# Ternary weights of a four-layer kernel prepared beside the first attention instead of ahead of it

## The reference

```python
x = norm(x + attention(x, wq, wk, wv, wo))          # causal, 32 query heads, 8 key heads, 16 wide, rotary
x = norm(x + ternary_ffn(x, w_fc, w_proj))          # 512 -> 2048 -> 512
x = norm(x + linear_attention(x, ...))
x = norm(x + experts(x, ...))                       # 16 experts, 2 per row, and a shared one

def ternarize_weights(w):                           # once for w_fc (2048x512), once for w_proj (512x2048)
    gamma = mean(abs(w))
    return sign(round(w / (gamma + 1e-6))) * gamma
```

## Time and profile before

| | us |
|---|---|
| median of 3 runs | 1881.5 (1878.66 to 1881.55) |
| the profiled execution | 1877.94 |
| its span in the profile | 1876.0 |
| mean granted TensorE clock | 0.952 |
| TensorE, VectorE, ScalarE, POOL busy | 86%, 64%, 50%, 22% |

### The profile page before, as it was taken

One profiled execution on the slowest core, in us unless ns is written; L12 is line 12 of the kernel. 1 busy time (PEld: TensorE's weight loads), 2 busy tenths in 40 slices (PEclk: granted clock), 3 DMA queues, 4 the chain that ended last, 5 costly groups with the idle time before them and its releaser, 6 DMA issues. The chain is left out here.

```text
span 1876.0 us, 33875 instructions
## 1 busy us (share of the span) xinstructions
PE 1616.8 (86%) x12714; PEld 817.7 (44%) x12714; DVE 1199.5 (64%) x2028; ACT 936.7 (50%) x1624; POOL 419.6 (22%) x503
## 2 busy tenths in 40 slices
PE   0488999978799998599996999777896999999997
PEld 0363333326333333244442454444553555666564
DVE  2556898844589885699975787699451243333277
ACT  4344677734467774577763666355221333333332
POOL 0070000116100002122222222255153111111154
PEclk9798999989899999899998999899897999999999
DMA  9000000000000000356454999543062564646344
GB/s 333 1 2 1 2 2 2 2 1 1 1 2 2 2 2 1 85 112 125 98 99 155 349 358 346 190 148 117 18 112 50 207 238 137 193 153 201 107 128 135
DMA packets 153970, 197.80 MB, mean 105 GB/s; under 512 B 94042, under 2 KB 97336, under 8 KB 151120
## 3 DMA queue, kind: packets, MB, share of 16 engines
q1 hardware_dynamic: 142288, 168.08, 29.1%
q0 software_dynamic: 7344, 20.73, 4.1%
q10 hardware_dynamic: 4176, 6.82, 1.0%
HBM read 184.94 MB, written 56.40 MB: 129 GB/s over the span
## 5 line engine op out<-in xcount | busy, mean ns | idle before, releaser
L713 ACT ACTIVATE attn_prob<-attn_ps_t 128x512 f32<-128x512 f32 x576 | 312.6, 595 | 151.2 <-PE attn_ps_t L667 149.7
L737 DVE TENSOR_REDUCE attn_mx<-attn_ps_s 128x2 f32<-128x1024 f32 (+3 forms) x304 | 342.7, 1163 | 42.9 <-PE attn_ps_s L648 39.4
L1985 PE MATMUL sparse_ps_g<-wgate,sparse_xT 128*128 128x352 f16 x1128 | 186.3, 316 | 3.6 <-DVE sparse_xT L2063 3.6
L680 PE MATMUL attn_ps_o<-attn_prob,V 128*32 128x256 f32 x2304 | 175.1, 389 | 0.8 <-ACT attn_oT L721 0.8
L1985 PEld LDWEIGHTS sparse_ps_g<-wgate,sparse_xT 128*128 128x128 f16 x1128 | 105.6, 99 | 75.2 <-DVE sparse_xT L2063 24.8
L1134 PE MATMUL lin_ps_z<-arena,lin_xT 128*128 128x512 f16 x576 | 134.0, 383 | 0.9 <-DVE lin_relu L1278 0.9
L900 PE MATMUL ffn_ps_fc<-wfcT,ffn_xT 128*128 128x512 f16 x512 | 115.8, 386 | 16.6 <-DMA ffn_xT<-ffn_x 16.6
L667 PE MATMUL attn_ps_t<-arena,KT 64*128 64x256 f16 x1152 | 112.5, 274 | 12.3 <-DMA arena<-attn_mT 6.5
L910 PE MATMUL ffn_ps_y<-wprojT,ffn_hT 128*128 128x512 f16 x512 | 115.1, 384 | 8.0 <-DMA ffn_hT<-ffn_h 8.0
L648 PE MATMUL attn_ps_s<-KT,arena 64*128 64x512 f16 (+3 forms) x768 | 115.8, 337 | 2.1 <-DVE attn_mx L737 2.1
L789 POOL TENSOR_TENSOR attn_o<-O,attn_o 128x512 f16<-128x512 f32 x16 | 18.5, 1158 | 442.3 <-ACT attn_o L726 442.3
(11 more groups left out here) (301 smaller groups left out, 3044.3 us busy)
## 6 DMA issues: line engine op xcount, KB each, us to landing
wgate<-gate_d SPq DMA_DIRECT2D x47, 1408.0 KB
wdown<-down_d SPq DMA_DIRECT2D x47, 768.0 KB
lin_sp_raw<-in_L_ffn_w_gate_up_dram SPq DMA_DIRECT2D x56, 352.0 KB, 5.3
gate_d<-lin_sp_parts SPq DMA_DIRECT2D x56, 352.0 KB, 4.9
y_d<-y SPq DMA_DIRECT2D x47, 256.0 KB
down_d<-lin_sp_parts SPq DMA_DIRECT2D x42, 256.0 KB, 5.1
lin_sp_raw<-in_L_ffn_w_down_dram SPq DMA_DIRECT2D x28, 256.0 KB, 5.2
prep_w_fc<-in_L_ffn_w_fc_dram SPq DMA_DIRECT2D x4, 1024.0 KB, 14.9
```

What stands on the lines that cost most here:

```text
L680: last = pe.matmul(ps_o[32 * jj:32 * jj + 32, 256 * half:256 * half + 256], V[:, kt, 4 * jg + jj, :], prob[(2 * q + jj // 2) % 4][:, half, ...
L713: act.activation(prob[g % 4][:, par, :, :], ps_t[:, (2 * g + par) % 3, :, :], ACT.Exp, scale=HD ** -0.5).then_inc(exp_done, 1)
L737: dve.tensor_reduce(mx[x % 2][:, c, :, at:at + per], ps_s[:, 2 * (r % 2):2 * (r % 2) + 2, 0:per * n].rearrange("p e (h k) -> p e h k", k=n ...
L1985: last = pe.matmul(ps_g[u][n][rows, :], xT[u][:, a, k, rows], w, start=(k == 0 and i == 0), stop=(k == KC - 1 and i == 2), skip_group_chec ...
```

## The change

The preparation block keeps only the tables, x and attention's weights. x is loaded by SP in four-tile pieces; the block waits for the first batch's half of it, the second half has a semaphore that the second projection waits for. ScalarE's wait for the weights is split: wq, wk, wv first, wo by itself.

In the first projection SP loads both ternary matrices in 16 chunks of 128x1024 (512 KB), with four buffers that lie in the place of `m.wfcT`; ScalarE sums the absolute values of two chunks per tile, as the last part of its list with a lag of 1; at the end TensorE adds the 16 sums and VectorE works out gamma and the thresholds.

In the first attention the chunks are loaded a second time, one per unit, by SP, after the unit's four small transfers. POOL compares each in three instructions (is less, is greater, difference), all sixteen chunks ahead of the rest of its stream. SP waits for each result, one unit later, and transposes it by DMA (two transfers for a chunk of w_fc, one for one of w_proj). The transposes and copies by TensorE and ScalarE are gone. The second batch's blocks are unchanged but for the wait for x.

```diff
@@ load_and_prepare
-                for c in range(4):
-                    sp.dma_start(w_fc[:, c * C4:(c + 1) * C4, :], fc_rows[:, c * C4:(c + 1) * C4, :]).then_inc(fc_in[c], 16)
-                for c in range(4):
-                    sp.dma_start(w_proj[:, c, :], proj_rows[:, c, :]).then_inc(proj_in[c], 16)
+                for t in range(0, TB, 4):
+                    sp.dma_start(m.X[:, t:t + 4, :], rows[:, t:t + 4, :]).then_inc(first_in, 16)
+                sp.dma_start(m.X[:, TB:NT, :], rows[:, TB:NT, :]).then_inc(m.later_in, 16)
+                sp.wait_ge(first_in, 32)
...
-                act.dma_start(w_o[:, :, :], d["L0_attn_wo"].rearrange("(k p) n -> p k n", p=P)).then_inc(wa_in, 16)
-                act.dma_start(m.X[:, :, :], d["L0_attn_x"].rearrange("b (t p) n -> p (b t) n", p=P)).then_inc(x_in, 16)
+                act.dma_start(w_o[:, :, :], d["L0_attn_wo"].rearrange("(k p) n -> p k n", p=P)).then_inc(wo_in, 16)
...
-                act.wait_ge(wa_in, 64)
+                act.wait_ge(wa_in, 48)
                 act.activation(m.wqkv_h[:, :, :], w_qkv[:, :, :], ACT.Copy, scale=WS).then_inc(hi_done, 1)
+                act.wait_ge(wo_in, 16)
                 act.activation(m.wo_h[:, :, :], w_o[:, :, :], ACT.Copy, scale=WS).then_inc(hi_done, 1)
...
+CHUNK = 2 * D
+CHUNKS = 2 * D * FF // (P * CHUNK)
@@ project_qkv
+                if b == 0:
+                    for c in range(CHUNKS):
+                        after(sp, abs_done, c - 3)
+                        rows = ternary_rows(d, c)
+                        sp.dma_start(raw[:, c % 4, :].rearrange("p (n k) -> p n k", n=rows.shape[1]), rows).then_inc(raw_in[c % 4], 16)
+                else:
+                    sp.wait_ge(m.later_in, 16)
...
+                def sums(t, u):
+                    if b == 0 and t == TB - 1:
+                        pe.wait_ge(abs_done, CHUNKS)
+                        pe.wait_ge(v_done, TB)
+                        pe.matmul(ps_v[:, 0:CHUNKS], m.ones[:, :], part[:, :], start=True, stop=True).then_inc(sum_done, 1)
...
-                run_tiles(act, TB, [(0, xhi), (2, vals), (2, qhi), (3, evac)])
+                def size(t, u):
+                    if b == 0:
+                        for c in range(t * CHUNKS // TB, (t + 1) * CHUNKS // TB):
+                            act.wait_ge(raw_in[c % 4], 16 * (c // 4 + 1))
+                            act.activation(raw[:, c % 4, :], raw[:, c % 4, :], ACT.Abs,
+                                           accum_out=part[:, c:c + 1]).then_inc(abs_done, 1)
+
+                unrolled(TB, [(0, of(xhi)), (2, of(vals)), (2, of(qhi)), (3, of(evac)), (1, of(size))])
@@ attend
             @block.gpsimd
             def _(pool):
+                def chunk(c):
+                    u, w = c % 2, c // (CHUNKS // 2)
+                    pool.wait_ge(raw_in[u], 16 * (c // 2 + 1))
+                    after(pool, turned[u], 16 * turns[c])
+                    pool.tensor_scalar(tern[u][:, :], raw[u][:, :], m.thr[:, 1, w:w + 1], None, ALU.is_lt).then_inc(neg_done, 1)
+                    pool.tensor_scalar(raw[u][:, :], raw[u][:, :], m.thr[:, 0, w:w + 1], None, ALU.is_gt).then_inc(neg_done, 1)
+                    pool.wait_ge(neg_done, 2 * c + 2)
+                    pool.tensor_tensor(tern[u][:, :], raw[u][:, :], tern[u][:, :], ALU.subtract).then_inc(tern_done, 1)
+
+                if ternary:
+                    for c in range(CHUNKS):
+                        chunk(c)
                 for kind, *a in ORDER:
...
+                def turn(sp, c):
+                    sp.wait_ge(tern_done, c + 1)
+                    columns = ternary_columns(m, c)
+                    for n, out in enumerate(columns):
+                        size = CHUNK // len(columns)
+                        sp.dma_start_transpose(out=out, in_=tern[c % 2][:, n * size:(n + 1) * size]).then_inc(turned[c % 2], 16)
+
                 for x, (qt, jg) in enumerate(UNITS):
                     sp.wait_ge(mt_done, x + 1)
                     for i in range(4):
                         at = qt * P + 32 * i
                         sp.dma_start(QT[3 * HD:P:64, 8 * jg:8 * jg + 8, at:at + 32],
                                      mT[x % 2][32 * i:32 * i + 16, :]).then_inc(mt_in[x % 2], 16)
+                    if ternary and x < CHUNKS:
+                        after(sp, tern_done, x - 1)
+                        rows = ternary_rows(d, x)
+                        sp.dma_start(raw[x % 2][:, :].rearrange("p (n k) -> p n k", n=rows.shape[1]), rows).then_inc(raw_in[x % 2], 16)
+                        if x:
+                            turn(sp, x - 1)
+                if ternary:
+                    turn(sp, CHUNKS - 1)
+                    for u in range(2):
+                        sp.wait_ge(turned[u], 16 * sum(len(ternary_columns(m, c)) for c in range(u, CHUNKS, 2)))
```

127 lines of the change are left out of this document (48 added, 79 removed).

## The result

The changed kernel took 1861.65 us in the median of four runs (1859.3 to 1864.9), the kernel before 1880.08 in the four beside them (1878.5 to 1881.6): a ratio of 0.9909 (95% interval 0.9889 to 0.9929), 18.4 us less. That is faster, by 0.9%, and 4.7 us above the 1857 of the forecast. A second measurement of the same kernel, the last of the experiments, gave 0.9942 (0.992 to 0.9965), which is 10.9 us. The forecast had 24, a ratio of 0.987.

A forecast was written before the change was run, and what follows sets the result against it. Barrier-ended stages bound the kernel: preparation is a gapless chain, attention a TensorE stage with POOL idle. -54.3 + 9.0 + 3.6 + 13.6 + 2 + 2 = -24.1 us, so 1857 us; range 1840 to 1878.

The forecast's parts named there:

- T: POOL's time per chunk in the first attention: two comparisons of 1.95 us and a subtraction of 2.3, 6.2 us (4.2 to 12.9).
- Preparation: Block before the first projection: it ends with wo's low part at 25.0 us, projection starts at 27.2 instead of 81.5, -54.3 us.
- Measuring in the ring: First projection: ScalarE's measuring lengthens each tile's chain of evacuation, x cast, POOL's rows and q cast; +9.0 us (0 to 13).
- Rival C: First projection: longer tiles drop TensorE to 1.2 GHz, costing 24 us in six tiles; 1881 us, no change; chance 0.06.
- rival B: First attention: POOL becomes the bound if T reaches about 12.7 us; slower than before, 1900 us at T = 15; chance 0.11.
- The comparison: POOL in the first attention: comparing 1024 columns with a scalar per partition takes 1.95 us, close under the cast's rate.
- rival A: POOL in the first attention: a comparison at nearly one column per cycle, 0.95 us, T 4.2; 1852 us; chance 0.17.
- SyncE's queue: First attention: unit 2's rows, and TensorE with them, wait behind chunk 0's compare and transpose; +3.6 us (1.6 to 22).
- one term for the clock: First attention: after the hole TensorE starts at the lower level, four us at half rate; +2 us (0 to 4).
- The end: End of the first attention: the last chunk's comparing delays POOL's low parts and TensorE's transpose; +13.6 us (11.6 to 20).
- The port: First attention: VectorE's small rows wait for POOL instructions at the shared port; +2 us (0 to 6); big reductions spared.

The follow-up runs named there:

- one_comparison: The changed kernel with the second comparison of each chunk left out (weights come out wrong); ratio 0.9891 to the kernel before, attention 288.9 us.
- ring_order: The changed kernel with ScalarE's two absolute sums per tile moved ahead of its cast of the queries; ratio 0.9874 to the kernel before, first projection 68.6 us.
- quarter_pieces: ring_and_table with each of POOL's three operations of a chunk cut into four of 256 columns; ratio 0.9736 to the kernel before, attention 270.9 us.
- ring_and_table: The changed kernel with both the edit of ring_order and that of sp_table; ratio 0.9745 to the kernel before, attention 274.2 us.
- sp_table: The changed kernel with chunk loads and turns given to SyncE's units by a table in which it never waits; ratio 0.9787 to the kernel before.

## Why the prediction was right or wrong

**Right in sign and range, and nearer in the total than in its parts.** 14.4 us came by the stages where 24.1 were forecast. That 1861.65 stands 4.7 us from 1857 owes something to luck: by the second measurement the gain is 10.9 us, less than half the 24 forecast, and the 7.5 us behind 1316 us in the first profile are spread. Of the 9.7 us missing in the stages, the comparison's price gave some 6, an estimate: in one_comparison 2.84 us less per chunk gave back 10.3 us of the attention, and T was 1.7 us too small.

*Preparation, right.* -55.3 against -54.3. The cast ran at 15.25 (forecast 15.5), wo's low part ended at 24.99 (25.0); the barrier was 1 us shorter.

*Measuring in the ring, right with its mechanism.* +10.2 against +9.0, tiles 8.33 us apart where 8.5 were named: five steps grew by 1.8 to 1.9 us each, where four had been put with 2.08. ring_order shows that only the place costs. Rival C, a TensorE falling to 1.2 GHz in the projection, did not happen: its window has a mean clock of 0.91, where before it had 0.90. Nor did rival B, which needed T at 12.7.

*The comparison, mis-sized: the step that failed.* "I take 1.95 with semaphores, close under the cast's rate" came out at 2.85 us, 2.8 ns a column, and T at 7.9 instead of 6.2. I leaned on the cast, one input like the comparison, and went below its 2.3 ns a column on the thought that a longer instruction spreads its fixed part. quarter_pieces lets one see the fixed part: 922 ns for 256 columns and 2848 for 1024 give 2.5 ns a column and some 280 ns fixed. There is one, but the comparison costs more per column than the cast does with its fixed part included. The Trainium skill's GPSIMD Engine Reference (Engine selection) has one input at roughly line rate and two inputs about twice as slow as on VectorE; in the trace the one-input comparison is the slower of the two, 2.85 us against 2.13 for the two-input subtraction of the same 1024 columns. The measurement decides, and rival A is out.

*SyncE's queue, right mechanism, two of its terms too small.* The chunk landed as forecast (POOL starts 11.05 us behind the stage's start, forecast 10.8). The hole before unit 2 is 5.84 us in place of 3.6, of which 1.7 is T and the rest the two turns, 2.61 us where 2.0 was put for both. one_comparison, with T at 5.1, has it at 3.1 us, and no later unit's rows waited in the queue for more than 0.2 us, so the queue was read rightly.

*What else made 13.1 us of the early loss: a second term too small, and one that was left out.* The held casts and maxima cost 3.7 us (6.8 in the two groups, 3.1 before), against 2. The remaining 3.6 (13.1 - 5.84 - 3.7) I put down to lower clock behind the holes and to shorter waits; no run takes them apart. The forecast had one term for the clock, 2 us, which the end alone used up. The rows of unit 3 come 6.9 us later than in the kernel before, of unit 4 9.8, of unit 5 12.3, and from there to the last it is 0.8 more. Between 120 and 134 us the mean clock is 0.79, as after a hole, and between 146 and 162 again 0.79; that second fall follows upon the cast of 2.05 us and three waits of 0.3 to 1.1 us, and the forecast had only one fall. In ring_order, whose casts fell elsewhere, there is no second fall (1.00 from 125 to 175 us) and the last rows came 2.4 us earlier.

*The end, right mechanism.* The wait is 15.2 us in place of 13.6, T again. From the last rows to the comparison's start it is 6.66 us (forecast 6.3). The other 2.5 of the 17.7 are probably the clock behind the hole, for which 2 had been put: the four key products take 0.61 us at 348.98 and 0.39 at 353.42. This was not taken apart.

*The port, right in kind.* The Trainium skill's page SBUF — State Buffer (Who interferes with whom) says of the shared pair of ports that whoever holds it keeps it for the whole instruction, that a cast may contend with GpSimd and that a reduction never does. The runs agree on the reductions, which took 1218 ns under 125 us of comparing and 1219 in the kernel before, and on POOL's subtraction, with whose end every cast and maximum begun inside it ended. They differ on the comparison, beside which casts begun in its middle were not held at all; the last section has the rows, and the measurement decides.

## What to carry to other kernels

Before work is moved to an idle engine, look for who stands behind it in every queue that it passes: here two positions in lists (SyncE's turn ahead of the next rows, POOL's last chunk ahead of the low parts) cost 26 us and one position on ScalarE 10, and moving lines, with the same work, gave these back. A wait on another engine belongs in a queue only where that engine has surely finished; load early and collect late. And small steps of VectorE on the critical path should not run beside long POOL instructions, which here held steps of 0.17 us for up to 2.1: write the wanted type in the step before, or cut POOL's instructions.

## What the runs showed of the hardware that I had not expected

- POOL compares 128x1024 with a scalar per partition in 2.85 us, whatever the width of the output (2848 ns for 16 and for 32 bits), but subtracts two tiles of that size in 2.13 us, again alike for 16 and 32 bits (2125 and 2132).
- Cut into 256 columns the comparison takes 0.92 us and the subtraction 0.67, some 0.28 and 0.18 us of which come with each instruction.
- A cast of 16 columns on VectorE, 0.17 us alone, took up to 2.05 us beside POOL. Over all traces the hold follows a pattern. All 23 casts and maxima that began inside a subtraction of 1024 columns, up to 1.89 us behind its start, ended within 0.04 us of its end. In a comparison of 1024 columns (2.85 us) there are two holds with a gap between: the eight begun 0.05 to 0.85 us behind its start all ended at 1.14 or 1.15 us (one begun at 0.03 was not held), the 24 begun between 0.96 and 1.80 us took their 0.17 to 0.18, and the 17 casts begun between 2.03 and 2.61 us ended with the instruction, while five maxima begun there were not held. What POOL does in that gap no run shows. A row of the first kind, from ring_and_table:

```profile
116.83 2.85 POOL L792 TENSOR_SCALAR attn_raw<-attn_raw,thr 128x1024 f32<-128x1024 f32 x1
116.88 1.09 DVE L751 CAST attn_top<-attn_mx 128x16 f16<-128x16 f32 x1
```

- The DMAs that turn 128x512 of a chunk landed 2.4 us after their issue in sp_table and 3.8 in the changed kernel, those of 128x1024 2.7 and 4.6 us (medians). Why stays open; in the changed kernel a load of 512 KB is issued right before each, which no run took apart.
- Tails came out near 57.2 or 58.5 us, and second attentions near 268 or 270, in kernels whose code there is the same. The tails go with TensorE's clock between 15 and 10 us before the stage's end: 0.94 to 0.98 in the four tails of 57.2 to 57.6 us, 0.71 or 0.72 in the four of 58.5, 0.80 in the one of 58.1. Why the clock falls there in some runs and not in others is open, and so nothing under 1.5 us was read from tails and second attentions.
